# Cross attention in a two-layer Perceiver: where the score and value products of neighbouring units stand in TensorE's order

## The chip, the cores and the metric

The kernel runs on one core of a Trainium2 chip. The metric is the device time of one execution, in microseconds (us). TensorE (PE) does the matrix products and is fed by weight loads (PEld); VectorE (DVE), ScalarE (ACT) and GpSimd (POOL) work beside it; SyncE (SP) issues most of the transfers. Each engine works through its own instructions in order, and semaphores order them across engines.

## The reference

Input `x` has 8 sequences of 64 tokens with 512 features, the context 8 sequences of 512 rows with 512 features. Six blocks follow each other, each with a residual: cross attention, linear attention and self attention with 31 experts in layer 0; cross attention, an mLSTM and 16 experts in layer 1. The change touches the two cross attentions only:

```python
# layer 0: 16 heads of 64
q = (layernorm(x) @ w_q);  k, v = split(context @ w_kv)
out = softmax(q * 64**-0.5 @ k.T) @ v @ w_out + b_out;  x += out * tanh(gate)
# layer 1: 16 heads of 32, a mask over context rows, biases
q = x @ Wq.T + bq;  k = context @ Wk.T + bk;  v = context @ Wv.T + bv
out = softmax(where(mask == 0, -1e20, q @ k.T) / sqrt(32)) @ v;  x += out @ Wo.T + bo
```

## The kernel before

**Units.** A cross attention is cut into 32 units, one for four heads of one sequence; a unit is named (c, u). In layer 0 there are 16 steps c (8 sequences, two halves of the heads) with two units each, in layer 1 8 steps with four units each. `self.plan` lists the units n = 0 to 31 in order and gives each the work that goes beside it.

**Four kinds of work on TensorE.** (1) `scores_tensor(n)`: the products of queries with keys, in banks 3 and 4. In layer 0 these are 8 matmuls on tiles of 64 rows by 64 columns of the array (L738), in layer 1 4 matmuls on tiles of 64 by 128 (L745). (2) `turn_tensor(n)`: 8 transposes of the probabilities by the whole array, 128 by 128, into banks 5 and 6 (L791). (3) `values_tensor(n)`: 32 matmuls of the turned probabilities with the values into bank 7 (L819), on tiles of 128 by 64 in layer 0 and 128 by 32 in layer 1. (4) `kv_tensor(c, g)`: a group, 12 matmuls of 128 by 128 by 512 columns (L648), which projects the context of a later step to an eighth of its keys or values, in one of banks 0 to 2 in turn. In layer 0 each unit has four groups (one `first`, one `second`, two `third`). In layer 1 a unit has one or two (`first`, sometimes `second`, no `third`): one each in units 0 to 2, 41 in units 3 to 28, so 15 of these have two and 11 have one, and none in units 29 to 31. Layer 1's units 1 and 2 also project two tiles of queries (L268). Near the end of each attention, where no groups are left, `project(i)` makes a tile of the output projection (L274): beside units 30 and 31 in layer 0, beside units 29, 30 and 31 in layer 1. These last units are those with `n >= beside`.

**Order on TensorE before.** In each unit: scores(n), queries, first, project, values(n - 1), second, turn(n), third. So the values of a unit come one unit behind its scores.

**The softmax of a unit.** DVE `softmax_vector(n)` waits for both score banks, takes the row maxima (L762; in layer 1 L759, which adds the mask and writes `prob`) and their negatives (L764, semaphore `topped`); ACT `softmax_scalar(n)` takes the exponentials (L781, `exped`); DVE takes a reciprocal (L769) and scales (L771, `normed`). `turn_tensor(n)` waits for `normed`, ACT `turn_scalar(n)` copies the turned banks (L799, `probT_a`), `values_tensor(n)` waits for that, DVE `values_vector(n)` reads bank 7 (L828 in layer 0, L831 in layer 1, `out_v`). In layer 1 the maxima of unit n + 1 also wait until the transposes of unit n have read the same half of `prob` (`turned`). DVE and ACT go through a unit as: softmax(n), first group's copy, values(n - 1) (DVE), splits of context tiles (L616, L621), second group's copy, turn copies (ACT), third. Copies of groups are L672, L674 (ACT) and L680 (DVE).

**What scores(n) waits for.** In layer 0 for the exponentials of unit n - 1 to have read the banks; in layer 1 for the maxima of unit n - 1 (`topped`) and for `qblk`, four small copies on POOL (`blocks_gpsimd`, L711, `blk`), which POOL may begin once scores(n - 2) are done. At a step's first unit it also waits for the copies of that step's keys, at its values for those of its values.

Of the kernel before, what the change touches and what calls it, by code (L numbers as in the profile page):

```python
# [81 lines left out]
def build_program(nc, A, out_dram):  # L82
# [404 lines left out]
    class CrossAttention:  # L487
# [360 lines left out]
        def attend_tensor(self, pe, project):  # L848

            units = len(self.units)  # L850
            beside = units - (2 if self.layer == 0 else 3)
            for n, c, u, first, second, third, splits in self.plan:
                self.scores_tensor(pe, n)
                self.queries_tensor(pe, self.queries_beside(c, u))
                for g in first:
                    self.kv_tensor(pe, *g)
                if n >= beside:
                    if n == beside:
                        pe.wait_ge(self.kv_v.sem, self.kv_v.at(self.evac[self.steps - 1, 2 * KT - 1][1]))
                    project(n - beside)  # L860
                if n >= 1:
                    self.values_tensor(pe, n - 1)
                for g in second:
                    self.kv_tensor(pe, *g)
                self.turn_tensor(pe, n)
                for g in third:
                    self.kv_tensor(pe, *g)
            if self.layer == 0:
                project(2)
            self.values_tensor(pe, units - 1)  # L870
# [2949 lines left out]
```

## Time and profile before

| What | Value |
|---|---|
| Device time, median of 3 runs | 1747.68 us (1747.32 to 1747.79) |
| The profiled execution: its own time | 1746.77 us |
| Its span, first to last instruction | 1744.9 us |
| Around the span | 1.87 us |
| PE busy | 1701.1 us (97%) |
| DVE, ACT, POOL busy | 979.7 (56%), 792.8 (45%), 237.6 (14%) |
| Chain that ended last, by engine | PE 92%, issue 2%, DVE 2% |
| Mean granted TensorE clock | 0.989 of full speed |
| Layer 0's units | about 66 to 523 us of the span |
| Layer 1's units | about 1075 to 1307 us of the span |

The profile is of one execution. Its times are counted from the start of the span. The ends of matmuls are modelled, so that neighbouring matmuls overlap in it, and an engine is called busy where it may be waiting for a few hundred nanoseconds: the starts are the surer numbers, and the distance from the first start of one kind of work to the first start of the next says how long TensorE was taken by it.

### The profile page before, as it was taken

To read this page: it belongs to the slowest core of one execution; us is meant where nothing else is said; L and a number is where in the kernel's file an instruction comes from. 1 tells how busy PE (TensorE), PEld (TensorE's weight loads), DVE (VectorE), ACT (ScalarE), POOL (GpSimd) and SP (SyncE) were. 2 spreads that over 40 slices of the span, in tenths; PEclk is the share of its full clock that TensorE was granted. 3 is DMA by queue.
4 is the path that set the end of the run, shared out by engine and by line. 5 is a ranking of instruction groups with operands and counts; after the bars stand their busy time and mean duration, and the time that the engine had idled before them with its cause. 6 is when DMAs were issued, how large, how long until landed. Compare 5 with 4: busy or idle time off the path is not lost.

```text
span 1744.9 us, 27121 instructions
## 1 busy us (share of the span) xinstructions
PE 1701.1 (97%) x10603; PEld 1294.9 (74%) x10603; DVE 979.7 (56%) x1999; ACT 792.8 (45%) x1564; POOL 237.6 (14%) x317
## 2 busy tenths in 40 slices
PE   7999999999999999999999999999999899999997
PEld 5577777777757766564999986676757778799996
DVE  4243344334336686522665665656554765598885
ACT  3333333333323345521555554445445443387774
POOL 0100000000001301313111112211100303122211
PEclk9999999999999999999999999999999999999998
DMA  6021110101042003034999972111231042599993
GB/s 250 4 94 35 39 48 26 49 25 71 27 157 97 1 1 120 26 122 164 347 387 389 384 255 80 40 53 37 80 122 49 25 196 105 195 353 364 363 366 106
DMA packets 43805, 246.52 MB, mean 141 GB/s; under 512 B 5801, under 2 KB 6305, under 8 KB 20624
## 3 DMA queue, kind: packets, MB, share of 16 engines
q1 hardware_dynamic: 31392, 216.63, 32.8%
q0 software_dynamic: 7664, 19.68, 4.1%
q10 hardware_dynamic: 4608, 8.33, 1.3%
q8 instruction: 89, 1.46, 0.3%
q14 instruction: 52, 0.43, 0.1%
HBM read 229.01 MB, written 16.13 MB: 140 GB/s over the span
## 4 chain that ended last, share of the span: by engine, by line
PE 92%; issue 2%; DVE 2%; ACT 1%; DMA 1%; POOL 1%; SPq 0%; POOLq 0%; DVEq 0%; ACTq 0%
PE bank L648 29%; PE bank L268 12%; PE bank L2372 7%; PE bank L274 5%; PE bank L791 3%; PE bank L3445 3%; PE bank L819 3%; PE bank L745 2%; PE bank L2923 2%; PE bank L1482 2%; PE bank L738 2%; PE bank L1166 2%; PE bank L1981 2%; PE bank L1983 2%; PE bank L1982 2%
## 5 line engine op out<-in xcount | busy, mean ns | idle before, releaser
L648 PE MATMUL bank<-split 128*128 128x512 f32 x2196 | 539.7, 398 | 1.5 <-ACT arena L674 1.5
L648 PEld LDWEIGHTS bank<-split 128*128 128x128 f32 x2196 | 402.0, 188 | 131.6 <-issue 21.7
L268 PE MATMUL bank<-arena,weights 128*128 128x128 f32 (+1 forms) x1032 | 136.4, 290 | 10.8 <-DMA weights<-in_L_xattn_w_kv 9.1
L268 PEld LDWEIGHTS bank<-arena,weights 128*128 128x128 f32 x1032 | 123.9, 193 | 24.2 <-issue 12.9
L762 DVE TENSOR_REDUCE small<-bank 128x1 f32<-128x512 f32 x64 | 43.9, 687 | 166.1 <-PE bank L738 166.1
L799 ACT COPY normed<-bank 128x512 f32<-128x512 f32 x128 | 68.9, 591 | 125.7 <-PE bank L791 125.7
L680 DVE COPY arena<-bank 128x512 f32<-128x512 f32 x76 | 52.4, 689 | 111.8 <-PE bank L648 111.8
L674 ACT COPY arena<-bank 128x512 f32<-128x512 f32 x76 | 44.5, 586 | 151.5 <-PE bank L648 113.3
L2372 PE MATMUL bank<-up_high_r,tok_r 128*128 128x352 f32 x512 | 108.2, 323 | 0.0
L274 PE MATMUL bank<-weights,arena 128*128 128x512 f32 x224 | 105.0, 620 | 0.9 <-issue 0.9
L781 ACT ACTIVATE normed<-bank,small 128x512 f32<-128x512 f32 x64 | 44.1, 689 | 124.0 <-DVE small L764 123.7
L2372 PEld LDWEIGHTS bank<-up_high_r,tok_r 128*128 128x128 f32 x512 | 86.5, 188 | 0.0
L268 PE MATMUL bank<-normed,weights 128*128 128x512 f32 (+1 forms) x216 | 83.3, 542 | 1.6 <-ACT normed L472 1.6
L274 PEld LDWEIGHTS bank<-weights,arena 128*128 128x128 f32 x224 | 42.9, 198 | 53.9 <-issue 53.0
L1917 POOL DMA_INDIRECT arena<-token_rows,arena x47 | 51.6, 1097 | 225.6 <-PE bank L1938 150.1
L1962 DVE TENSOR_TENSOR slot_r<-weights,normed_r 128x512 fp32r<-128x512 f32 x124 | 77.2, 685 | 0.2 <-ACT normed_r L1957 0.2
L2692 ACT ACTIVATE arena<-bank,cols 128x128 f32<-128x128 f32 x124 | 35.4, 368 | 88.4 <-PE bank L268 88.4
L759 DVE CUSTOM_DVE_ANT_0 arena<-bank,arena 128x512 f32<-128x512 f32 x64 | 44.3, 692 | 55.5 <-PE bank L745 55.4
L2355 DVE TENSOR_TENSOR long_slot_r<-weights,up_high_r 128x1408 fp32r<-128x1408 f32 x40 | 63.1, 1620 | 16.9 <-ACT up_high_r L2350 16.9
L268 PEld LDWEIGHTS bank<-normed,weights 128*128 128x128 f32 x216 | 41.5, 196 | 38.3 <-issue 34.0
L1957 ACT CAST normed_r<-weights 128x512 fp32r<-128x512 f32 x124 | 68.0, 640 | 0.5 <-ACT arena L2175 0.5
L1355 POOL TENSOR_TENSOR arena<-arena 128x2048 f32<-128x2048 f32 x1 | 3.6, 3602 | 470.4 <-DVE arena L1253 470.4
(404 smaller groups left out, 3142.5 us busy)
## 6 DMA issues: line engine op xcount, KB each, us to landing
weights<-in_L_ffn_re_w SPq DMA_DIRECT2D x62, 1024.0 KB, 10.7
weights<-in_L_w SPq DMA_DIRECT2D x20, 1408.0 KB, 11.9
arena<-in_ctxT SPq DMA_DIRECT2D x24, 1024.0 KB, 4.9
arena<-in_L_w SPq DMA_DIRECT2D x12, 1408.0 KB, 11.8
weights<-in_L_w_full SPq DMA_DIRECT2D x10, 1280.0 KB, 10.2
weights<-in_L_ffn_sw SPq DMA_DIRECT2D x9, 1024.0 KB, 4.8
expert_out<-arena ACTq DMA_DIRECT2D x31, 256.0 KB, 8.2
arena<-in_L_w_full SPq DMA_DIRECT2D x6, 1280.0 KB, 10.9
```

What stands on the lines that cost most here:

```text
L268: s = pe.matmul(out, w[:, k, j0:j0 + m], rhs(k), start=(k == 0), stop=(k == KT - 1))
L274: s = pe.matmul(out, lhs(k0 + k), w[:, k, j0:j0 + n], start=(start and k == 0), stop=(stop and k == KT - 1))
L648: s = pe.matmul(bank[:, :], still, moving, start=(n == 0), stop=(n == len(order) - 1))
L680: dve.tensor_copy(dst, self.kv_bank(c, g)[:, :]).then_inc(self.kv_v.sem, 1)
L791: last = pe.transpose(banks[5 + s][:, t * P:(t + 1) * P], self.prob[s][:, t * P:(t + 1) * P], ident[:, :])
L799: act.copy(self.probT[s], blocks(banks[5 + s][:, :], CTX // P)).then_inc(self.probT_a.sem, 1)
L819: last = pe.matmul(banks[7][r:r + d, o:o + SEQ], self.v[c % len(self.v)][:, t, f:f + d], self.probT[s][:, t, i * SEQ:(i + 1) * SEQ], start ...
L1957: act.copy(self.w2_high[ex % 2][:, m, :], w2.view[:, m, :]).then_inc(self.raised("w2_high"), 1)
L1962: dve.tensor_tensor(w2.rounded[:, m, :], w2.view[:, m, :], self.w2_high[ex % 2][:, m, :], ALU.subtract).then_inc(self.raised("w2_low"), 1)
L2355: dve.tensor_tensor(w.rounded_flat[:, c], w.flat[:, c], high, ALU.subtract).then_inc(up_low.sem, 1)
L2372: s = pe.matmul(banks[2 + 2 * j + z][:, 0:half], tok1_r[still][:, k, :], moving[:, a:a + half], start=False, stop=(k == KT - 1 and still = ...
L3445: s = pe.matmul(bank[:, :], w[:, k, j:j + P], z[:, k, :], start=(n == 0), stop=(n == len(order) - 1))
```

## The change

Only TensorE's order changes; what each engine computes and every other queue stay the same. In layer 0, for units 1 to 29, values(n - 1) is moved from behind the first group to just behind scores(n). In layer 1 scores(0) goes ahead of the loop, and in each unit scores(n + 1) is issued behind values(n - 1) and ahead of the second group and turn(n); units 29 to 31 and their `project` come under this order too.

```diff
@@ attend_tensor
             units = len(self.units)
             beside = units - (2 if self.layer == 0 else 3)
+            if self.layer == 1:
+                self.scores_tensor(pe, 0)
             for n, c, u, first, second, third, splits in self.plan:
-                self.scores_tensor(pe, n)
+                adjoin = self.layer == 0 and 1 <= n < beside
+                if self.layer == 0:
+                    self.scores_tensor(pe, n)
+                if adjoin:
+                    self.values_tensor(pe, n - 1)
                 self.queries_tensor(pe, self.queries_beside(c, u))
                 for g in first:
                     self.kv_tensor(pe, *g)
...
-                if n >= 1:
+                if n >= 1 and not adjoin:
                     self.values_tensor(pe, n - 1)
+                if self.layer == 1 and n + 1 < units:
+                    self.scores_tensor(pe, n + 1)
                 for g in second:
                     self.kv_tensor(pe, *g)
                 self.turn_tensor(pe, n)
```

## Rows read from the trace of the kernel before

**Rows 1.** Busy time by engine in the stretches of the two attentions.

```profile
66.00:514.00 448.00, 448.00 (x2965) 335.18 (x2966) 182.92 (x410) 151.87 (x317) 7.22 (x5) 1.00 0.15 56
...
1075.00:1308.00 233.00, 231.88 (x1977) 157.12 (x1976) 138.92 (x411) 114.19 (x237) 33.86 (x128) 1.00 0.17 62
```

**Rows 2.** Timeline of PE in layer 0: start, us, engine, line, operation.

```profile
67.03 5.76 PE L648 MATMUL bank<-split 128*128 128x512 f32 x24
72.63 1.03 PE L791 MATMUL bank<-ident,normed 128*128 128x128 f32 x8
...
79.05 1.09 PE L738 MATMUL bank<-arena 64*64 64x512 f32 x8
80.07 3.03 PE L648 MATMUL bank<-split 128*128 128x512 f32 x12
83.03 1.15 PE L819 MATMUL bank<-normed,arena 128*64 128x64 f32 x32
84.11 3.02 PE L648 MATMUL bank<-split 128*128 128x512 f32 x12
86.97 1.03 PE L791 MATMUL bank<-ident,normed 128*128 128x128 f32 x8
87.76 5.70 PE L648 MATMUL bank<-split 128*128 128x512 f32 x24
93.39 1.09 PE L738 MATMUL bank<-arena 64*64 64x512 f32 x8
```

**Rows 3.** Weight loads grouped by line, layer 0: busy, mean ns, idle before.

```profile
L738 PEld LDWEIGHTS bank<-arena 64*64 64x64 f32 x256 | 6.7, 131 | 11.5 <-issue 11.5
```

**Rows 4.** The chain that ended last, where twelve groups follow each other.

```profile
1032.84 32.66 PE bank L648 x144
```

**Rows 5.** Timeline of PE in layer 1, from one turn to a second group.

```profile
1117.16 1.09 PE L791 MATMUL bank<-ident,arena 128*128 128x128 f32 x8
1118.18 1.13 PE L745 MATMUL bank<-arena 64*128 64x512 f32 x4
1119.24 3.04 PE L648 MATMUL bank<-split 128*128 128x512 f32 x12
1122.21 0.65 PE L819 MATMUL bank<-normed,arena 128*32 128x64 f32 x32
1122.79 3.02 PE L648 MATMUL bank<-split 128*128 128x512 f32 x12
```

**Rows 6.** Timeline of PE at the end of layer 0's units.

```profile
506.12 7.13 PE L274 MATMUL bank<-weights,arena 128*128 128x512 f32 x16
...
514.26 1.10 PE L791 MATMUL bank<-ident,normed 128*128 128x128 f32 x8
515.19 7.03 PE L274 MATMUL bank<-weights,arena 128*128 128x512 f32 x16
```

**Rows 7.** Timeline of all engines in layer 1, between two turns.

```profile
1249.68 1.03 PE L791 MATMUL bank<-ident,arena 128*128 128x128 f32 x8
1249.88 0.69 DVE L680 COPY arena<-bank 128x512 f32<-128x512 f32 x1 [2.42 <-PE bank L648]
1250.32 1.07 ACT L799 COPY normed<-bank 128x512 f32<-128x512 f32 x2 [4.37 <-PE bank L791]
...
1251.82 0.69 DVE L759 CUSTOM_DVE_ANT_0 arena<-bank,arena 128x512 f32<-128x512 f32 x1 [1.25 <-PE bank L745]
...
1253.41 0.15 DVE L764 TENSOR_SCALAR small<-small 128x1 f32<-128x1 f32 x1
...
1254.64 0.49 DVE L771 TENSOR_SCALAR arena<-arena,small 128x512 f32<-128x512 f32 x1
...
1255.23 1.09 PE L791 MATMUL bank<-ident,arena 128*128 128x128 f32 x8
```

**Rows 8.** Timeline of all engines in layer 1, where POOL adds a bias.

```profile
1101.81 1.42 POOL L2835 TENSOR_TENSOR x_tok<-x_tok,rows 128x512 f32<-128x512 f32 x1 [4.72 <-POOLq L2833]
...
1102.47 1.06 DVE L771 TENSOR_SCALAR arena<-arena,small 128x512 f32<-128x512 f32 x1
```

## The prediction, as it was put on record before the change was run

> **What bounds the kernel now.** I read the busy time by stretch first. While layer 0's units run, TensorE is busy for 448.00 us of 448.00, and while layer 1's run, for 231.88 of 233.00; DVE and ACT are busy for well under two thirds [rows 1]. So in both attentions nothing that another engine does is on the path, but for about one microsecond at the end of layer 1. Time can be won there only by giving TensorE less to do, or by letting its work follow itself more closely. Busy does not mean at work, though: the ends of matmuls are modelled. So the second view is TensorE's timeline, read by the distances between starts [rows 2, 5]. The reader is to see there that the same twelve matmuls of a group take different times by what stands ahead of and behind them.
>
> **What a neighbour costs.** Where twelve groups follow each other, 144 matmuls take 32.66 us [rows 4], 0.227 each, so a plain group is 2.72. In layer 0:
> - A group behind scores and ahead of values lasts from 80.07 to 83.03, 2.96: 0.24 more.
> - One behind values and ahead of a turn lasts from 84.11 to 86.97, 2.86: 0.14 more.
> - Two behind a turn and ahead of scores last from 87.76 to 93.39, 5.63: 0.19 more than two plain ones (5.44).
> - Two behind scores and ahead of a turn, in unit 0 where there are no values yet, last from 67.03 to 72.63, 5.60: 0.16 more.
>
> All four are in [rows 2].
>
> So leaving a group for a small tile costs about 0.08 more than leaving it for the turn (0.24 against 0.16, both behind scores), and coming back into a group costs around 0.1. The scores' weight loads show the same from the other side: they sat idle for 11.5 us in 32 units, 0.36 each, for nothing that the profile names [rows 3].
>
> **Layer 0: one way in and out of small tiles fewer.** No instruction is added or removed; 32 value matmuls move over 12 of a group. Before, a unit has scores, group, values, group, turn; the two groups take 2.96 + 2.86 = 5.82. After, it has scores, values, group, group, turn; the groups then stand together behind values and ahead of a turn: 5.44 + 0.14 = 5.58. The scores' distance to what follows is 1.02 and the values' is 1.08 [rows 2]; I keep both. Saved: 0.24 a unit; unit 0's pair, 5.60, would make it 0.22. Units 1 to 29 change: 29 x 0.24 = 7.0 us.
>
> What no row shows is values right behind scores. Bounds: if it is easier than from a group (both are small tiles), the 0.08 for entering goes too, so up to 29 x 0.08 = 2.3 more is saved. If the values' loads had to sit idle once more as long as the scores' do, 0.36 [rows 3], the unit would lose 0.12, 29 x 0.12 = 3.5 us slower in layer 0. I take the middle, no extra: the 1.02 behind scores holds where a group follows, which is a change of tile as well.
>
> The Trainium skill bears on this (TensorEngine Tiling (Array Packing), Key Properties): changing the tiling mode, not just the tile, drains TensorE. Scores on 64 by 64 and values on 128 by 64 are two modes, so by it nothing of that 2.3 is won, and the sum stays at my 7.0; the idle 0.36 agrees with a drain, though no row shows this pair.
>
> Do new waits come? values(n - 1) needs turned probabilities that ACT copies behind turn(n - 1); two whole groups still lie between, over 5 us, and two copies take 1.07 [rows 7]. turn(n) has the same work ahead of it after the scores, less 0.24: 6.9 us before (80.07 to 86.97), and the softmax chain in layer 1, which is longer by the mask, takes 3.31 (below). Banks 0 to 2 are reused three groups later, so a group that ends 1 us later in its unit has a copy of 0.69 and several us to spare. Priced at nothing; DVE and ACT hide it.
>
> **Layer 1: scores move away from between turn and group.** All 31 scores but the first move ahead by a turn. Before: turn to scores 1.02, scores to group 1.06, group 2.97, values 0.58 [rows 5]. After: turn to group, then values, scores, and then a second group or the turn.
> - Turn to group: in layer 0 a turn behind a group hands over to a group after 0.79 [rows 2]. A turn behind small tiles is 0.06 longer (1.09 against 1.03 [rows 2, 5]), and here it stays behind small tiles: 0.85, against 1.02 before. 0.17 less.
> - The group now stands behind a turn and ahead of values: 2.72 + 0.19 = 2.91 against 2.97 [rows 2, 5]: 0.06 less.
> - Values to scores: values are left after 0.58 towards a group [rows 5]; the same towards scores, by the same reading as above. Scores are left after 1.06, also towards a turn.
>
> Sum 0.23 a unit, for units 3 to 28: 26 x 0.23 = 6.0. Five more units have a projection behind the scores. Behind a turn instead it starts after 0.93 and takes 7.03, where behind scores it takes 7.13 [rows 6], so 0.09 + 0.10 each, 0.9 in all. Against it: scores(1) now part unit 0's group from its turn, 0.15 (0.08 for the small tile and 0.06 for the turn). And the first output projection waits for the copy of the very last group: such a copy starts 0.20 after the turn's start and takes 0.69 [rows 7], so it lands at 0.9 or so where TensorE would be ready at 0.85: with the signal I put 0.15 in. Layer 1: 6.0 + 0.9 - 0.3 = 6.6 us. Bounds: the 0.06 of the group is the least sure, since DVE and ACT will do other work beside it than they do beside layer 0's; without it, 1.6 us less is won.
>
> **Layer 1's new waits.** In program order each scores(n + 1) now stands ahead of turn(n), and waits for the maxima of unit n; behind it are turn(n), for which ACT's copies wait, and all later work. Take the start of turn(n - 1) as 0 in a unit with one group, the tightest. The group starts at 0.85, values at 3.76, scores(n + 1) at 4.34, turn(n) at 5.40. ACT's copies of turn(n - 1) start at 0.64 and take 1.07 [rows 7]: done at 1.7, ahead of the values at 3.76. DVE can begin the maxima at 0.64 too, or at 0.89 behind a group's copy; the second negative maximum is ready 1.74 later (1251.82 to 1253.56) and the second scaled half 3.31 later (to 1255.13) [rows 7]. So the maxima are there at 2.6, 1.7 us before scores(n + 1) ask, and the probabilities at 4.2, 1.2 us before the turn. Before, the turn started at 1255.23, 0.1 after them: the chain gets room, because scores are there a turn earlier.
>
> One row stands out: beside POOL's bias addition of 1.42 the DVE scaling took 1.06 and not 0.49 [rows 7, 8]. There are four such additions, and 0.57 fits in the 1.2. The Trainium skill (SBUF — State Buffer, Who interferes with whom) has a port pair that DVE and GpSimd take in turns, the loser blocked for a whole instruction; this row agrees, and by it the most is one such block at a time, so the sum stays.
>
> POOL's four small copies for unit n + 1 may begin once scores(n - 1) are done, now as before two scores earlier, and unit n's keys were copied many groups ago. Transfers keep their conditions and shift with TensorE. Behind each attention the work starts from its last output tile and moves forward by what is won.
>
> **The sum.** 7.0 + 6.6 = 13.6 us. From the profiled execution's 1746.77 (span 1744.9) that is 1733.2; it lies 0.9 below the median of the runs, from which the sum gives 1747.68 - 13.6 = **1734.1 us**.
>
> **Rivals.**
> - *Scores and values adjoin without the price of entering.* For: both use partial tiles of the array, with columns in halves. Against: rows differ, 64 against 128. Gains up to 2.3 more, in layer 0: 1731.8.
> - *Values behind scores cost as much as was won,* so that layer 0 gives nothing. For: no row has the pair, and the idle of 0.36 may return. 1747.68 - 6.6 = 1741.1; with the whole 0.36, 1744.6.
> - *Layer 1 gives nothing,* because scores(n + 1) or turn(n) wait a little. For: the turn met its probabilities with 0.1 to spare before. Against: 1.7 and 1.2 us of room. 1747.68 - 7.0 = 1740.7.
> - *Slower: TensorE stands behind the maxima in layer 1.* If DVE's queue (group's copy, values, split, mask) holds back the maxima of unit n, scores(n + 1) block turn(n) and with it the rest. It decides from 13.6 / 12 = 1.1 us of wait in each of the 12 or so units with one group, that is maxima 2.8 us later than I reckon. At 1.5 us each: 1734.1 + 18 = 1752.
> - *The change doesn't tell:* what a switch costs is not in the place but in the start marks of the records. Then 1747.7. Against: unit 0's two groups took 5.60, where later ones took 5.82.
>
> **How the numbers follow.** Chances: forecast 0.66, its own range 1732.5 to 1736.5 (the 1.6 of layer 1 and half of the entering); cheaper entering 0.11; layer 0 nothing 0.09; layer 1 nothing 0.07; no change 0.03; slower 0.04. The predicted time is the likeliest. The range 1731 to 1741.5 leaves out the last two cases and a little of the others. A difference of 0.2% is 3.5 us, about what a measurement of this kernel can tell: faster 0.93, same 0.03, slower 0.04.
>
> **What would show it.** In layer 0, scores to values 1.02, values to group 1.08, two groups 5.58, and units 0.24 shorter. In layer 1, turn to group 0.79 to 0.85, group 2.91, values to scores 0.58, scores to turn or group 1.06, and no idle of TensorE in front of L745 or L791. The prediction is wrong if L819's distance from L738 grows over 1.1, or if the timeline has waits of L745 for DVE.

## The result, and the profile after

| | Before | After |
|---|---|---|
| Device time, median of 6 runs | 1745.4 us (1739.42 to 1747.79) | 1730.32 us (1729.39 to 1736.48) |
| The profiled execution, its own time | 1746.77 | 1730.11 |
| Its span | 1744.9 | 1728.2 |
| First scores to last values, layer 0 | 456.15 | 450.35 |
| First scores to last values, layer 1 | 231.70 | 224.79 |
| The rest of the span | 1057.0 | 1053.1 |

The ratio after to before is 0.9933, 95% interval 0.9917 to 0.995, so about 11.7 us faster; the two medians differ by 15.1 us, since each rests on six runs that spread over 7 to 8 us. The three runs of before that were shown ahead of the prediction took around 1747.7 us, three later ones 1739.42 to 1743.48. Two executions of the experiments below, one of 2433.72 us in e1 (mean granted clock 0.653) and one of 2126.76 us in e3 (0.75), are in none of the ratios. The two profiled spans differ by 16.7 us, but only 5.80 + 6.91 = 12.7 of it lies in the two attentions.

The lengths in the table are distances between the starts of these rows. In the timeline of the kernel before:

```profile
66.01 0.66 PE L738 MATMUL bank<-arena 64*64 64x512 f32 x4
...
522.16 1.04 PE L819 MATMUL bank<-normed,arena 128*64 128x64 f32 x28
...
1075.26 1.13 PE L745 MATMUL bank<-arena 64*128 64x512 f32 x4
...
1306.96 0.65 PE L819 MATMUL bank<-normed,arena 128*32 128x64 f32 x32 [0.73 <-ACT normed L799]
```

In that of the kernel after:

```profile
65.55 1.09 PE L738 MATMUL bank<-arena 64*64 64x512 f32 x8
...
515.90 1.15 PE L819 MATMUL bank<-normed,arena 128*64 128x64 f32 x32
...
1070.72 1.13 PE L745 MATMUL bank<-arena 64*128 64x512 f32 x4
...
1295.51 0.65 PE L819 MATMUL bank<-normed,arena 128*32 128x64 f32 x32 [0.73 <-ACT normed L799]
```

TensorE's timeline of one unit in layer 0 after the change, to be held against [rows 2]:

```profile
78.59 1.09 PE L738 MATMUL bank<-arena 64*64 64x512 f32 x8
79.61 1.15 PE L819 MATMUL bank<-normed,arena 128*64 128x64 f32 x32
80.69 5.78 PE L648 MATMUL bank<-split 128*128 128x512 f32 x24
86.31 1.03 PE L791 MATMUL bank<-ident,normed 128*128 128x128 f32 x8
87.10 5.70 PE L648 MATMUL bank<-split 128*128 128x512 f32 x24
92.73 1.09 PE L738 MATMUL bank<-arena 64*64 64x512 f32 x8
```

Scores to values 1.02, values to groups 1.08, and the two groups, now in one row of 24, take 5.62 (80.69 to 86.31) where they took 2.96 + 2.86. A unit is 14.14 long (78.59 to 92.73) and was 14.34 (79.05 to 93.39).

Layer 1, to be held against [rows 5]: the turn of one unit (1112.57), then a whole unit with two groups, the second of them behind the scores, up to its turn (1120.86):

```profile
1112.57 1.09 PE L791 MATMUL bank<-ident,arena 128*128 128x128 f32 x8
1113.42 3.01 PE L648 MATMUL bank<-split 128*128 128x512 f32 x12
1116.36 0.65 PE L819 MATMUL bank<-normed,arena 128*32 128x64 f32 x32
1116.94 1.13 PE L745 MATMUL bank<-arena 64*128 64x512 f32 x4
1118.00 3.02 PE L648 MATMUL bank<-split 128*128 128x512 f32 x12
1120.86 1.04 PE L791 MATMUL bank<-ident,arena 128*128 128x128 f32 x8
```

The turn hands over after 0.85, where the scores took their place after 1.02; the group takes 2.94 against 2.97, values 0.58 and scores 1.06. In the timeline there is no idle time ahead of any of them, and the only wait of TensorE for another engine in all of layer 1's units is the one that was there before, 0.7 us at the last values. The room of the softmax is in the other engines' rows of the same unit:

```profile
1113.26 1.08 ACT L799 COPY normed<-bank 128x512 f32<-128x512 f32 x2 [1.04 <-PE bank L791]
...
1113.40 0.69 DVE L759 CUSTOM_DVE_ANT_0 arena<-bank,arena 128x512 f32<-128x512 f32 x1 [0.45 <-PE bank L791]
...
1114.99 0.15 DVE L764 TENSOR_SCALAR small<-small 128x1 f32<-128x1 f32 x1
...
1116.23 0.49 DVE L771 TENSOR_SCALAR arena<-arena,small 128x512 f32<-128x512 f32 x1
```

The second negative maximum is there at 1115.14 and the scores that wait for it start at 1116.94: 1.8 us of room. The probabilities are ready at 1116.72; a turn could follow the scores at 1118.00 at the earliest, 1.3 us later. Before, that room was 0.1 [rows 7]. (A turn waits for the two halves of the probabilities one after the other, and asks for the second only at its fifth transpose, so these numbers are on the safe side.) Measured the same way over units 3 to 28, the scores have 1.40 to 1.80 us of room. The turns of the eleven units with one group have 0.90 to 1.26 us, but for unit 3 with 0.53, where one of POOL's bias additions lies beside the scaling.

### The profile page after: what moved, and what is told of

It is laid out like the page before. It is cut to its first block, busy times and chain, and to the rows that moved or that the text cites. A ratio compares the mean times of both kernels' runs of the same rounds, so it can differ in the third digit from the quotient of the medians.

```text
span 1728.2 us, 27121 instructions
## 1 busy us (share of the span) xinstructions
PE 1679.0 (97%) x10603; PEld 1290.0 (75%) x10603; DVE 980.5 (57%) x1999; ACT 791.9 (46%) x1564; POOL 234.0 (14%) x317
## 3 DMA queue, kind: packets, MB, share of 16 engines
q8 instruction: 89, 1.46, 0.4%
## 4 chain that ended last, share of the span: by engine, by line
PE 92%; DVE 3%; DMA 2%; ACT 1%; issue 1%; POOL 1%; SPq 0%; POOLq 0%; DVEq 0%; ACTq 0%
PE bank L648 29%; PE bank L268 12%; PE bank L2380 7%; PE bank L274 5%; PE bank L791 3%; PE bank L3453 3%; PE bank L819 3%; PE bank L745 2%; PE bank L2931 2%; PE bank L1490 2%; PE bank L738 2%; PE bank L1174 2%; PE bank L1989 2%; PE bank L1991 2%; PE bank L1990 2%; PE bank L1547 1%
## 5 line engine op out<-in xcount | busy, mean ns | idle before, releaser
L648 PE MATMUL bank<-split 128*128 128x512 f32 x2196 | 530.4, 396 | 1.3 <-ACT arena L674 1.3
L680 DVE COPY arena<-bank 128x512 f32<-128x512 f32 x76 | 52.5, 691 | 120.8 <-PE bank L648 120.8
L621 DVE TENSOR_TENSOR split<-arena,split 128x512 fp32r<-128x512 f32 x92 | 61.6, 708 | 30.4 <-ACT split L616 30.1
L819 PEld LDWEIGHTS bank<-normed,arena 128*64 128x64 f32 (+1 forms) x1792 | 44.3, 125 | 36.1 <-issue 35.1
L1953 DVE COPY arena<-bank 128x512 f32<-128x512 f32 x31 | 21.4, 691 | 81.1 <-PE bank L1946 81.0
```

The source lines that it names most:

```text
L621: dve.tensor_tensor(low, src, high, ALU.subtract).then_inc(self.low.sem, 1)
L648: s = pe.matmul(bank[:, :], still, moving, start=(n == 0), stop=(n == len(order) - 1))
L680: dve.tensor_copy(dst, self.kv_bank(c, g)[:, :]).then_inc(self.kv_v.sem, 1)
L819: last = pe.matmul(banks[7][r:r + d, o:o + SEQ], self.v[c % len(self.v)][:, t, f:f + d], self.probT[s][:, t, i * SEQ:(i + 1) * SEQ], start ...
```

## The experiments

Every row of this table is one kernel: its stage lengths, from first scores to last values, and the rest of its span are those of its profiled execution, the ratio is that of all its executions but the two named above. The stage lengths repeat to some hundredths in every kernel that leaves a stage as it was, while the rest of the span varies by itself. e1 to e4 were run on one chip and e5 to e8 on another, each beside before on the same chip. Edits are shown against the kernel before unless the text says otherwise; `...` stands for lines left out.

| Kernel | Layer 0 | Layer 1 | Rest of span | Ratio to before (95%) |
|---|---|---|---|---|
| before | 456.15 | 231.70 | 1057.0 | 1 |
| after | 450.35 | 224.79 | 1053.1 | 0.9933 (0.9917 to 0.995) |
| e1 layer 0 alone | 450.35 | 231.70 | 1052.4 | 0.9946 (0.9929 to 0.9964) |
| e2 layer 1 alone | 456.15 | 224.77 | 1054.9 | 0.9955 (0.9938 to 0.9973) |
| e3 after again | 450.35 | 224.77 | 1047.5 | 0.9918 (0.9895 to 0.9941) |
| e4 three together | 448.08 | 223.90 | 1051.2 | 0.9898 (0.9879 to 0.9917) |
| e5 values ahead of scores, layer 0 | 450.35 | 231.68 | 1051.1 | 0.9967 (0.9953 to 0.9981) |
| e6 values behind scores, layer 1 | 456.15 | 227.50 | 1053.4 | 0.9979 (0.9965 to 0.9993) |
| e7 values moved, not adjoining | 454.41 | 231.69 | 1053.4 | 1.0006 (0.9994 to 1.0017) |
| e8 values in two halves | 465.23 | 231.65 | 1055.7 | 1.0074 (1.0051 to 1.0096) |

### Each layer's change alone, and the whole again

For layer 0 alone the scores stay at the head of the unit in both layers, and only the values move (shown against the changed kernel):

```diff
-            if self.layer == 1:
-                self.scores_tensor(pe, 0)
...
-                if self.layer == 0:
-                    self.scores_tensor(pe, n)
+                self.scores_tensor(pe, n)
...
-                if self.layer == 1 and n + 1 < units:
-                    self.scores_tensor(pe, n + 1)
```

> The change in layer 0 alone; layer 1 keeps its order of before. Theory (each way in and out of small tiles has its price, and layer 0 has one fewer per unit): from the first scores to the last values layer 0 takes 450.3 us, as after the whole change (before 456.1), and layer 1 stays at 231.7: 5.8 us less in all. Rival (a good part of the measured gain lies outside the two attentions and comes with the change, the spans differ by 16.7 us while the attentions give 12.7): more than 5.8 less, by up to 4 us again outside the attentions.

For layer 1 alone `adjoin` is off (against the changed kernel too):

```diff
-                adjoin = self.layer == 0 and 1 <= n < beside
+                adjoin = False
```

> The change in layer 1 alone; layer 0 as before. Theory: layer 0 stays at 456.1 us, layer 1 goes from 231.7 to 224.8, 6.9 us less in all, and with the run of layer 0 alone it adds up to the whole, 12.7. Rival (layer 1 gains through the softmax chain, which begins a turn earlier, and not through TensorE's switches): units whose turn did not wait before would gain nothing, so well under 6.9.

> The changed kernel once more, beside the others on the same chip. Theory: both attentions the same to 0.1 us as in the first profile (450.3 and 224.8), the rest of the span differing by several us with the granted clock of the stretches outside them; the ratio to before at 12.7 us less, 0.9927. Rival (something of the change reaches work outside the attentions): the rest differs by the same 4 us from before again.

Layer 0 alone gives 5.80 us in layer 0 and nothing in layer 1; layer 1 alone gives 6.93 in layer 1 and nothing in layer 0. They add up to the 12.7 of the whole. Almost all of layer 1's gain is on TensorE's own timeline and not in the longer room of the softmax. Units gain whose turn had no need of more room: in unit 6 the probabilities were ready 3 us ahead of the turn before, and it is 8.29 long from turn to turn (1112.57 to 1120.86) where it was 8.49 (1117.16 to 1125.65). Only two short waits inside turns went away, where the second half of the probabilities was still being scaled. One is in unit 0 of before:

```profile
1079.18 1.23 PE L791 MATMUL bank<-ident,arena 128*128 128x128 f32 x8
1079.20 0.49 DVE L771 TENSOR_SCALAR arena<-arena,small 128x512 f32<-128x512 f32 x1
...
1080.34 1.13 PE L745 MATMUL bank<-arena 64*128 64x512 f32 x4
```

From this turn to the scores are 1.16 us, where it is 0.96 or 0.97 for the other turns behind a group. The other is in unit 3 (1103.08 to 1104.16, 1.08 where it is 1.02 for the others behind values). Together they are about 0.25 of the 6.9 us.

The rest of the span does not follow the change: with the same changed program it was 1053.1 once and 1047.5 once, and the other changed kernels, which differ only inside the attentions, lie from 1051.1 to 1055.7. The executions that were not profiled say the same, if the stage lengths of the profile are taken off their spans, which is an estimate. The 22 executions of before that ran beside e5 to e8 (spans 1735.9 to 1745.5) leave 1048.1 to 1057.7, and the eleven of the changed kernel that count in its two ratios (1722.6 to 1734.5) leave 1047.5 to 1059.4. The ratio of layer 0 alone, 0.9946, is a little better than 5.8 / 1743.9 would make it (0.9967, just outside its interval); the whole, 12.7 / 1743.9 or 0.9927, lies in both of its intervals. I take the stage lengths as the gain, and the remainder of each ratio as that scatter.

### All small tiles in one row

```diff
+            self.scores_tensor(pe, 0)
             for n, c, u, first, second, third, splits in self.plan:
-                self.scores_tensor(pe, n)
                 self.queries_tensor(pe, self.queries_beside(c, u))
                 for g in first:
                     self.kv_tensor(pe, *g)
...
                     project(n - beside)
+                for g in second:
+                    self.kv_tensor(pe, *g)
                 if n >= 1:
                     self.values_tensor(pe, n - 1)
+                if n + 1 < units:
+                    self.scores_tensor(pe, n + 1)
-                for g in second:
-                    self.kv_tensor(pe, *g)
                 self.turn_tensor(pe, n)
```

> In both layers values(n - 1), scores(n + 1) and turn(n) stand in one row behind the first and second groups, so that all groups of a unit follow each other behind the turn. Theory: in layer 0 the way back into a group from a small tile goes too, a unit from 14.14 to 14.02 us, 3.5 us over 29 units, less up to 1 us at the first output projection, which then waits for the last group's copy; in layer 1 0.09 for each of the 15 units with two groups, 1.3 us. 3.8 us less than the changed kernel, 16.5 less than before. Rival (scores or the turn wait once they stand at the unit's end, behind maxima and exponentials of the unit): idle of TensorE in front of L791 or L738, and no gain over the changed kernel.

TensorE's timeline in layer 0 of this kernel:

```profile
98.57 1.15 PE L819 MATMUL bank<-normed,arena 128*64 128x64 f32 x32
99.65 1.09 PE L738 MATMUL bank<-arena 64*64 64x512 f32 x8
100.67 1.09 PE L791 MATMUL bank<-ident,normed 128*128 128x128 f32 x8
101.52 11.15 PE L648 MATMUL bank<-split 128*128 128x512 f32 x48
112.60 1.15 PE L819 MATMUL bank<-normed,arena 128*64 128x64 f32 x32
```

All four groups stand in one row of 48, and a unit is 14.03 long (98.57 to 112.60) against 14.14. Layer 0 is 2.27 us shorter than after the change and layer 1 0.87 to 0.89: 3.1 in all against an expected 3.8, for a unit gave 0.11 and not 0.12, and layer 1's units 0.06 and not 0.09. The wait at the first output projection was reckoned in, and is there further on in the same timeline:

```profile
486.91 1.13 PE L274 MATMUL bank<-weights,arena 128*128 128x512 f32 x2 [0.78 <-DVE arena L680]
```

The rival, a wait for maxima or probabilities, is not there: TensorE waits for no other engine elsewhere in layer 0, and in layer 1 only at the last values, as before. Its two attentions are the shortest of all the kernels here. Its ratio to before is 0.9898 (0.9879 to 0.9917). On the same chip, the median of its four executions is 1725.72 us, that of the changed kernel's five 1726.25, and that of before's eleven 1743.9. That it beats the changed kernel rests on the 3.1 us of the stages alone: the two medians differ by 0.5 us, and the intervals of the two ratios overlap.

### Order, distance and dose

Values ahead of scores in layer 0:

```diff
+                adjoin = self.layer == 0 and 1 <= n < beside
+                if adjoin:
+                    self.values_tensor(pe, n - 1)
                 self.scores_tensor(pe, n)
...
-                if n >= 1:
+                if n >= 1 and not adjoin:
                     self.values_tensor(pe, n - 1)
```

> Layer 0 alone: values(n - 1) directly ahead of scores(n) in place of directly behind. Layer 1 as before. Theory (what counts is that the two adjoin, not their order): a unit of 14.12 to 14.14 us, 5.8 to 6.4 us less than before in all. Rival (leaving scores for values is cheap or dear by itself, since the tiles share their columns): a unit differs from 14.14 by more than 0.05.

Layer 0 took 450.35 us, the same to the hundredth as with values behind scores. So neither way between 64 by 64 and 128 by 64 is cheaper or dearer than the other.

The same pair in layer 1, in the order of layer 0's change (`adjoin` for layer 1, values directly behind scores, both still behind the turn):

```diff
+                adjoin = self.layer == 1 and 1 <= n < beside
                 self.scores_tensor(pe, n)
+                if adjoin:
+                    self.values_tensor(pe, n - 1)
...
-                if n >= 1:
+                if n >= 1 and not adjoin:
                     self.values_tensor(pe, n - 1)
```

> Layer 1 alone: scores stay behind the turn of the unit before, and values(n - 1) come directly behind scores(n), as layer 0 was changed. Theory: what counts is again that small tiles adjoin; some 5.5 us less than before, a little under the 6.9 of the order that was chosen. Rival (the order chosen gains by giving the softmax chain a turn more): here the values stand 2.0 us behind the turn's start where ACT's copies end at 1.7, and the chain from scores to turn has as little room as before, so waits at L819 or L791 eat the gain.

Layer 1 went from 231.70 to 227.50: 4.2 us of the 5.5 expected. Here waits ate a part, as the rival had it: five of them, all at the values. The waits of TensorE in layer 1, summed (us, times, longest), and one of them in the timeline:

```profile
PE bank L819 <- ACT normed L799: 1.6, 5, 0.3
```

```profile
1229.90 1.13 PE L745 MATMUL bank<-weights,arena 64*128 64x512 f32 x4
1231.36 0.65 PE L819 MATMUL bank<-normed,weights 128*32 128x64 f32 x32 [0.33 <-ACT normed L799]
```

By the starts, each of the five costs about 0.4 us (1229.90 to 1231.36 is 1.46, where scores hand over after 1.06 elsewhere), 2.0 in all. 4.2 + 2.0 is 6.2, somewhat more than the 5.5 reckoned. Adjoining gains in both orders. The order that was chosen for layer 1 leaves ACT's copies a whole group of time, so these waits do not come, and it also moves the scores of the last three units, which this kernel leaves where they were; how the remaining 0.7 divides was not tried.

Values moved as far, but the other way, to stand between the second group and the turn of layer 0:

```diff
+                moved = self.layer == 0 and 1 <= n < beside
-                if n >= 1:
+                if n >= 1 and not moved:
                     self.values_tensor(pe, n - 1)
                 for g in second:
                     self.kv_tensor(pe, *g)
+                if moved:
+                    self.values_tensor(pe, n - 1)
                 self.turn_tensor(pe, n)
```

> Control in layer 0: values(n - 1) move as far as in the change, but the other way, behind the second group and ahead of the turn, so that they do not adjoin scores. Layer 1 as before. Theory: the small tiles stay apart from each other and only the way out of the values changes, into a turn in place of a group; 0.07 a unit, 2.1 us less than before. Rival (any move that lets two groups follow each other gains the whole): 5.8 us less.

Here too two groups follow each other, but the values stand apart from the scores:

```profile
91.80 1.09 PE L738 MATMUL bank<-arena 64*64 64x512 f32 x8
92.82 5.75 PE L648 MATMUL bank<-split 128*128 128x512 f32 x24
98.50 1.15 PE L819 MATMUL bank<-normed,arena 128*64 128x64 f32 x32
99.58 1.09 PE L791 MATMUL bank<-ident,normed 128*128 128x128 f32 x8
100.43 5.72 PE L648 MATMUL bank<-split 128*128 128x512 f32 x24
106.08 1.09 PE L738 MATMUL bank<-arena 64*64 64x512 f32 x8
```

The stage gains 1.74 us, near the 2.1 expected and far from 5.8; the ratio, 1.0006, does not show even that: 1.74 would be 0.9990, just below its interval, and the rest of the program scatters by more. Two groups in a row are not what pays; fewer parted small tiles are.

And one parting more, the values in two halves with a group between (the argument picks the pair of heads, and the semaphore is raised by the second half; these lines of `values_tensor` are not shown):

```diff
+                halved = self.layer == 0 and 1 <= n < beside
                 if n >= 1:
-                    self.values_tensor(pe, n - 1)
+                    self.values_tensor(pe, n - 1, (0,) if halved else None)
                 for g in second:
                     self.kv_tensor(pe, *g)
+                if halved:
+                    self.values_tensor(pe, n - 1, (1,))
                 self.turn_tensor(pe, n)
```

> Dose in layer 0: the 32 value matmuls in two halves, 16 where they stood and 16 behind the second group, so one way in and out of small tiles more. Layer 1 as before. Theory: 0.28 a unit, 8.2 us slower than before. Rival (the price is in the count of matmuls or in the values' start, not in the switches): no more than 0.05 a unit.

```profile
96.13 0.69 PE L819 MATMUL bank<-normed,arena 128*64 128x64 f32 x16
96.74 3.02 PE L648 MATMUL bank<-split 128*128 128x512 f32 x12
99.69 0.69 PE L819 MATMUL bank<-normed,arena 128*64 128x64 f32 x16
100.31 1.09 PE L791 MATMUL bank<-ident,normed 128*128 128x128 f32 x8
```

The halves take 0.61 and 0.62, together 1.23 where the whole took 1.08, and the group between them 2.95. Layer 0 is 9.08 us longer than before, 0.31 a unit, against the 8.2 expected, with the same matmuls. Ratio 1.0074 (1.0051 to 1.0096). Before, a unit of layer 0 has two stretches of small tiles, scores and values. One stretch fewer took 5.8 us away, one more added 9.1: the time goes up and down with the count of stretches, the matmuls being the same. The count is not all, though. With two stretches as before, the control gave 1.74 us by setting the values against the turn in place of a group. With one stretch as after the change, all small tiles in one row gave 2.27 more by setting the turn behind it.

## Why the prediction was right, point by point

**What bounds.** That TensorE's timeline alone sets both attentions held: all nine kernels besides before moved by what their switches changed, and the few waits that came are counted above.

**The price of a neighbour.** Right, and it carried over to pairs that no row had shown. The open one, values right behind scores, cost what the prediction took: scores hand over after 1.02 whatever follows (78.59 to 79.61). The rival of a cheap way between two partial tilings is refuted by the same rows, and the mirrored order gave the same 450.35.

What the prediction had only as 0.36 us of idle weight loads can be read more closely where two kinds of work meet. In before, in layer 1:

```profile
1249.45 1.02 PEld L791 LDWEIGHTS bank<-ident,arena 128*128 128x128 f32 x8
1249.68 1.03 PE L791 MATMUL bank<-ident,arena 128*128 128x128 f32 x8
...
1250.64 0.30 PEld L745 LDWEIGHTS bank<-arena 64*128 64x128 f32 x4 [0.17 <-issue]
1250.64 1.13 PE L745 MATMUL bank<-arena 64*128 64x512 f32 x4
```

The turn's first weight load starts 0.23 us ahead of its first matmul, beside the group that is still running; that of the scores starts with its first matmul. It is so throughout the units of both profiles, before and after. Where both neighbours use the whole array, the first load runs ahead, by 0.23 from a group to a turn and by 0.03 from a turn to a group, unless it has to wait for a copy, as at layer 1's first output projection. Wherever the tile form changes, also from scores to values and from values to scores, it does not run ahead at all. A turn differs from a group in its columns and its operands too, but not in its tiles, and there the loads do run ahead; so it is the tile form that goes with the price. How much of the price is the way in and how much the way out, no run separates.

**Layer 0: 7.0 predicted, 5.8 measured.** The term that was mis-sized is the pair of groups, 5.44 + 0.14 = 5.58: it measured 5.62. The bound from unit 0 (5.60, so 0.22 a unit) was the nearer row. I had carried the 0.14 over from a group that stood a group later. Why the pair costs 0.04 more was not found. That DVE's maxima now lie beside it does not settle it, since unit 0's pair begins beside them too and took 5.60, and in e6 a pair between values and turn of layer 1 took 5.58 (1231.94 to 1237.52). That the excess lies in that pair is what the rows show: in all 29 units it took 5.62, and 29 x 0.20 is the 5.8.

**Layer 1: 6.6 predicted, 6.9 measured.** A unit came out 0.23 shorter, as taken: the turn of unit 3 to that of unit 28 took 183.22 us before and 177.38 after, 5.84 over 25 units. About 0.25 of the 0.3 more than predicted is the two short waits inside turns of before, shown above, which the prediction did not count. The first output projection waits as reckoned: it starts 0.95 behind its turn, just after the copy of the last group has ended (1276.52 to 1277.21), where a group starts after 0.79 (86.31 to 87.10, above). It did not get the 0.10 shorter that the prediction gave each projection; those behind it did (3.70 and 3.60 in these rows):

```profile
1276.32 1.03 PE L791 MATMUL bank<-ident,arena 128*128 128x128 f32 x8
1277.27 3.70 PE L274 MATMUL bank<-weights,arena 128*128 128x512 f32 x8
...
1282.54 1.09 PE L791 MATMUL bank<-ident,arena 128*128 128x128 f32 x8
1283.47 3.60 PE L274 MATMUL bank<-weights,arena 128*128 128x512 f32 x8
```

**The new waits.** Reckoned room 1.7 us for the maxima and 1.2 for the probabilities, measured 1.40 to 1.80 and, in units with one group, 0.53 to 1.26. The slower rival needed the maxima 2.8 us late and was far off. POOL's bias additions lengthened two scalings by more than the 0.57 reckoned, to 1.24 us (at 1097.16) and 1.09 (at 1102.60) from 0.49. Even so they brought no wait: the turn of unit 3 starts at 1098.94, 0.53 after the first of them has ended.

**The sum and the time.** 13.6 predicted, 12.7 measured in the attentions, about 11.7 by the ratio. The time was predicted as 1734.1 from a base of 1747.68, the median of three runs; the ratio makes 1747.68 x 0.9933 = 1736.0 of that base. The median of the six runs after is 1730.32, 0.7 below the range, beside a median of 1745.4 before. What the prediction left out is that the rest of the program scatters by several us between executions, in both kernels. How near the time came is therefore in part luck: layer 0's gain was put 1.2 us too high and layer 1's 0.3 too low, which partly cancel, and the rest of the program scatters by more than the 0.9 that is left.

## What to carry to other kernels

On an engine that never waits, read the distances between starts, not the busy time: what stands next to an instruction can cost 5 to 9% of a group of twelve (0.14 to 0.24 of 2.72 us) without any wait in the profile. Put work on small tiles of the array side by side, whatever its order, and count the stretches of small tiles between those of the whole array. Here, in layer 0, one stretch fewer was worth 0.20 us a unit and one more cost 0.31. Before moving work ahead of a wait, reckon the room from the rows of the waiting chain; here 0.5 us or more was left in every unit, and the move brought no wait.

## What the runs showed of the hardware that was not expected

**Weight loads and tile forms.** From one kind of whole-array work to another the first weight load ran ahead of the first matmul, by 0.23 us from a group to a turn and 0.03 from a turn to a group; at every change of tile form within the units it did not. The rows are above, at the price of a neighbour.

**The clock outside the attentions.** The time outside the attentions varies from execution to execution of the same instructions, 1047.5 to 1057.0 us in these profiles, and part of it goes with the granted clock. The busy time of the stretch behind layer 1's cross attention, before, and for the changed kernel in its second profile, e3 (column behind POOL: PEclk):

```profile
1307.00:1744.00 437.00, 419.00 (x2208) 359.19 (x2208) 311.90 (x500) 251.49 (x367) 79.59 (x56) 0.97 0.59 212
```

```profile
1292.00:1722.00 430.00, 409.15 (x2184) 352.58 (x2176) 314.27 (x498) 251.01 (x367) 76.60 (x56) 0.99 0.60 215
```

437 us at 0.97 against 430 at 0.99: TensorE's busy time differs by 9.9 us for nearly the same instructions. These shares are means of two levels. In all, the clock stood at its lower level, 1.2 GHz, for 36.9 us of the span in the profile of before, for 13.9 in that of the change, and for 10.1 in that of e3. One such stretch of before, and the same work in e3, where the clock stayed at 2.4 GHz:

```profile
1387.20:1390.60 3.40, 3.40 (x8) 1.85 (x7) 3.29 (x13) 2.57 (x4) 1.68 (x2) 0.50 0.00 0
```

```profile
1368.60:1372.00 3.40, 3.40 (x10) 1.49 (x9) 3.31 (x9) 2.57 (x4) 1.90 (x2) 1.00 0.00 0
```

A tile of projection lies in both, and takes 4.86 us in the first (1387.71 to 1392.57) and 3.43 in the second (1368.62 to 1372.05). Ahead of it TensorE had waited 2.6 us for DVE and 2.3 for POOL in both executions, so these waits alone do not decide whether the clock falls; what does was not tried. In the attentions themselves the granted clock was 1.00 in all ten profiles, which fits their lengths repeating to some hundredths.
